# Attention scores from turned gathered rows, head products loaded over ScalarE's queue, and scatters that wait for landings

## The chip, the core and the metric

The kernel runs on one core of one Trainium2 chip. A core has TensorE (PE), VectorE (DVE), ScalarE (ACT), GpSimd (POOL) and SyncE (SP), each with its own instruction stream. They meet over semaphores; transfers go through 16 DMA engines. The metric is the device time of one execution in microseconds (us), as a median over runs.

## What is computed

Four graph layers one after the other on 3125 nodes of 64 values and 100000 edges sorted by destination: attention over four heads, two Chebyshev convolutions, messages with edge values, and a second kind of attention over 2048 nodes. The change touches the first layer, its preparation, and a re-sorting of the edge values for the third.

```python
h = jnp.maximum(_layernorm(x, axis=-1), 0.0)
# layer 0
Q = (h @ Wq).reshape(n, H, D)
K = (h @ Wk).reshape(n, H, D)
V = (h @ Wv).reshape(n, H, D)
score = jnp.einsum('ehd,ehd->eh', Q[src], K[dst]) / np.sqrt(D)
attn = jax.nn.softmax(score, axis=1)
m = V[src] * attn[:, :, None]
h_new = jax.ops.segment_sum(m, dst, num_segments=n)
...
# layer 2
message = jax.nn.relu(node_feats[edge_index[1]] + edge_feats)
message_reduce = jax.ops.segment_sum(message, edge_index[0], num_segments=num_nodes)
```

## The kernel before

The score of an edge and head is the product of the source's row h with a row that depends on the destination alone, h[dst] times a 64x64 matrix per head. `front` (the preparation) computes these head products for all nodes, 25 blocks of 128. In each block TensorE turns the rows (L661), ScalarE copies them (L584), TensorE multiplies (L667), and ScalarE and VectorE split the result into three bf16 parts (L588, L434, L590, L439). They go to the table `r3` in memory, node by node. TensorE and VectorE count edges for the later layers in the same loop.

`attend` then handles 100 items: 1000 edges each, eight tiles of 125, whose destinations lie in a window of nodes. Its loop does two items per turn, and most buffers (`spot`, `edges`, `rwin`, `hsrc`) have two slots. Per item:

- SyncE reads two numbers of the item (L760, L761) and issues four loads: `spot`, the item's numbers (L763), `edges`, its table (L766), `rwin`, the window of `r3`, 120 pieces of 512 bytes (L779), and `dstrow`, the destinations of 1000 edges on each of 120 partitions (L772).
- POOL issues eight indirect gathers, each 125 rows of h, into `hsrc` (L807). It waits first for `ao_free`, which TensorE raises when it has weighed the item that lay in the slot.
- VectorE builds `there`, a one-hot of 120x1000 that says which window row each edge wants (L850, threshold L843). TensorE multiplies it with the window (L1031), which lays the head products of 125 edges times 256 in PSUM. VectorE multiplies these with the gathered rows (L875) and adds up over 64 values (L883); ScalarE adds up four of the sixteen sums of a half item by copies with an accumulator, each followed by a read of it (L968). After the softmax (L913, L917, L982 on ScalarE, L926 to L928) L930 lays the weights into `AO`.
- TensorE weighs the gathered rows with `AO` (L1004), sixteen records of f32 products, and counts destinations by sources (L1049) from one-hots of VectorE (`hot`, L866) and ScalarE (`lo`, L958, L961). VectorE adds the counts to a large matrix (L890). Every second item TensorE projects the sums (L1018), from `U`, which ScalarE copied (L950).

After the last item an extra set of `edges` and gathers is loaded that nobody uses.

`spread` runs the rest of layer 0 and layer 1: it exchanges pairs of blocks of the count matrix (up to 1802 us in the profile), then four propagations of 25 blocks, each block ending in L1680, then the end of the layer. Beside that the edge values for layer 2 are re-sorted: 40 chunks of two halves; for each half SyncE loads the edge values, the pairs and the places (`bring_half`: L701, L704 with 1250 pieces of 8 bytes, L706), and POOL scatters them in ten indirect transfers of 125 rows (L1254) into `sorted_edges`. After every run of five POOL raises `run` and waits for `go`, which SyncE raises in `follow` (L1188) after three increments of another semaphore. SyncE loads a half anew as soon as all ten scatters of it have landed (L1194). After chunk 23 SyncE also waits for the third propagation and then reloads part of the count matrix (`again`, 1.6 MB each, twelve times, L1200) after every chunk. Layer 2 then takes 42 message items, four groups each with one activation L1572; ScalarE loads 1 MB of sorted rows per item, when the chunk is ready. Layer 3 follows from 3177 us on.

## Time and profile before

| what | us |
|---|---|
| median of 3 runs | 3109.45 |
| lowest and highest | 3109.2, 3112.74 |
| span of the profiled execution | 3529.8 |
| preparation, in the profile | 0 to about 200 |
| attention | about 200 to 1576 |
| exchange of pairs | 1576 to about 1802 |
| propagations and the layer's end | 1802 to 2415 |
| messages of layer 2 | 2415 to 3172 |
| layer 3 | 3177 to 3530 |

Times inside the program come from one execution that the hardware profiler recorded, 420 us longer than the median. A row's busy time is the sum over its instructions, and instructions of an engine overlap a little at their ends. "issue" is time in which an engine waited for nothing that the profile shows; "remote" is a wait whose end it can't name.

### The profile page before, as it was taken

The numbers are of one execution on the slowest core, as the hardware profiler recorded it, in microseconds if no ns is written. First come the engines' busy times: TensorE is split into PE (matmuls) and PEld (weight loads), VectorE is DVE, ScalarE is ACT, GpSimd is POOL, SyncE is SP. The second block draws the span as 40 slices with busy tenths as digits, with TensorE's granted clock in tenths as the row PEclk, the third lists the DMA queues.
The fourth block names the chain that finished last, engine by engine and source line by source line (L and its number), as shares of the span: only waits on it lengthen the run. The fifth ranks groups of instructions, "written<-read, shape, count | busy, mean of one in ns | idle before, by whom it ended". The sixth has DMA issues, their size and how long they took to land. (4 is left out here: it accounts for less than half of the span.)

```text
span 3529.8 us, 59565 instructions
## 1 busy us (share of the span) xinstructions
PE 1964.1 (56%) x16222; PEld 1430.6 (41%) x16222; DVE 2235.0 (63%) x4872; ACT 1128.3 (32%) x3658; POOL 1615.5 (46%) x1665
## 2 busy tenths in 40 slices
PE   6844555555555555545766556564545445564487
PEld 5723333333333333334344435453434434554222
DVE  7877777777777777754521112134547557987899
ACT  1144555444444444533210111000001001117544
POOL 1055555555555555553666666645666562000000
PEclk9955555555555555556767677675657657985699
DMA  7912121121212222236222222215544432220000
GB/s 240 364 40 45 42 45 43 43 43 44 45 40 45 42 45 41 45 88 224 65 49 50 50 50 48 60 44 154 147 132 145 127 81 84 85 82 0 0 0 9
DMA packets 399309, 267.13 MB, mean 76 GB/s; under 512 B 321456, under 2 KB 349293, under 8 KB 399073
## 3 DMA queue, kind: packets, MB, share of 16 engines
q1 hardware_dynamic: 306278, 87.81, 11.6%
q10 hardware_dynamic: 41472, 118.96, 9.3%
q0 software_dynamic: 51488, 59.40, 6.7%
q8 instruction: 47, 0.77, 0.1%
q14 instruction: 24, 0.20, 0.0%
HBM read 158.59 MB, written 107.47 MB: 75 GB/s over the span
## 5 line engine op out<-in xcount | busy, mean ns | idle before, releaser
L1254 POOL DMA_INDIRECT sorted_edges<-r_load,r_to x800 | 818.6, 1023 | 544.9 <-SPq L1188 310.2
L807 POOL DMA_INDIRECT hsrc<-h,edges x808 | 775.7, 960 | 593.8 <-PE ps L1004 362.4
L1004 PE MATMUL ps<-AO,hsrc 125*64 125x64 f32 x1616 | 195.9, 316 | 309.9 <-remote 254.3
L1049 PE MATMUL ps<-hot,lo 125*128 125x400 bf16 (+2 forms) x1000 | 272.8, 455 | 100.5 <-DVE hot L866 79.9
L1004 PEld LDWEIGHTS ps<-AO,hsrc 125*64 125x64 f32 x1616 | 180.0, 224 | 345.8 <-issue 345.8
L1031 PE MATMUL ps<-rwin,there 120*125 120x256 bf16 x800 | 183.2, 404 | 235.3 <-DVE there L850 220.0
L875 DVE TENSOR_TENSOR prod<-ps,hsrc 125x1024 f32<-125x1024 f32 x200 | 244.3, 1222 | 105.1 <-issue 101.0
L1572 ACT ACTIVATE w_work<-w_work 128x384 f32<-128x384 f32 (+1 forms) x160 | 85.8, 536 | 701.5 <-DVE w_work L1773 530.4
L866 DVE TENSOR_SCALAR hot<-ramp,small 125x400 bf16<-125x400 int16 x800 | 211.9, 322 | 148.0 <-issue 142.7
L1426 PE MATMUL ps<-R 128*128 128x64 bf16 x3000 | 156.6, 218 | 184.5 <-DVE R L1762 115.9
L1031 PEld LDWEIGHTS ps<-rwin,there 120*125 120x125 bf16 x800 | 145.1, 209 | 274.1 <-issue 274.1
L1680 DVE TENSOR_REDUCE c_red<-ps 128x64 f32<-128x192 f32 x100 | 35.7, 357 | 346.1 <-remote 220.5
L968 ACT ACTIVATE prod<-prod 125x64 f32<-125x64 f32 x800 | 194.3, 245 | 166.8 <-issue 89.4
L958 ACT ACTIVATE lo<-ramp,edges 125x128 bf16<-125x128 int16 x808 | 246.8, 388 | 0.0
L1366 PE MATMUL ps<-R,A 128*128 128x192 bf16 x1250 | 164.0, 294 | 99.3 <-issue 98.7
L1426 PEld LDWEIGHTS ps<-R 128*128 128x128 bf16 x3000 | 132.2, 114 | 206.5 <-DVE R L1762 137.5
L1049 PEld LDWEIGHTS ps<-hot,lo 125*128 125x128 bf16 x1000 | 132.4, 137 | 195.0 <-DVE hot L866 97.9
L1436 PE MATMUL ps<-w_work 128*128 128x64 bf16 x1000 | 142.3, 213 | 112.0 <-DVE R L1781 76.7
L1773 DVE TENSOR_TENSOR w_work<-ps,w_work 128x384 f32<-128x384 f32 (+1 forms) x160 | 91.4, 571 | 170.8 <-remote 160.9
L883 DVE TENSOR_REDUCE small<-prod 125x12 f32<-125x768 f32 x200 | 189.9, 949 | 3.4
L1366 PEld LDWEIGHTS ps<-R,A 128*128 128x128 bf16 x1250 | 134.4, 117 | 129.2 <-issue 124.3
L1436 PE MATMUL ps<-R,w_work 128*128 128x64 bf16 x2000 | 156.0, 215 | 42.8 <-issue 42.5
(412 smaller groups left out, 4187.1 us busy)
## 6 DMA issues: line engine op xcount, KB each, us to landing
w_work<-sorted_edges ACTq DMA_DIRECT2D x42, 1000.0 KB
r_load<-in_edge_attr_dram SPq DMA_DIRECT2D x80, 312.5 KB
dstrow<-dst_rows SPq DMA_DIRECT2D x101, 234.4 KB
sorted_edges<-A ACTq DMA_DIRECT2D x10, 2000.0 KB, 9.7
A<-counts SPq DMA_DIRECT2D x12, 1600.0 KB
counts<-A ACTq DMA_DIRECT2D x4, 4000.0 KB, 29.8
sorted_edges<-A ACTq DMA_DIRECT2D x15, 1000.0 KB, 9.5
hsrc<-h,edges POOLq DMA_INDIRECT x808
```

Source lines behind the costliest of these rows:

```text
L807: g.indirect_dma_start(out=hsrc[:, s, t, :], out_offset=None, in_=S.h0[:, :], in_offset=bass.IndirectOffsetOnAxis(ap=edges.bitcast(I32)[:, ...
L866: v.tensor_scalar(hot[0:TP, t, :], S.ramp[0:TP, OFF[t] * NB:OFF[t] * NB + SK], key[:, t:t + 1], None, ALU.is_equal).then_inc(q["hot"], 1)
L875: v.tensor_tensor(prod[0:TP, :].rearrange("p (t h f) -> p t h f", t=HT, h=H), S.ps[0:TP, hf * 1024:(hf + 1) * 1024].rearrange("p (t h f) - ...
L958: op = nc.scalar.activation(lo[0:TP, s, t, :], S.ramp[0:TP, 0:P], ACT.Square, bias=edges[0:TP, s, 3, t:t + 1])
L968: op = nc.scalar.activation(prod[0:TP, c * D:(c + 1) * D], prod[0:TP, c * D:(c + 1) * D], ACT.Copy, accum_out=score[:, hf * HT * H + c:hf ...
L1004: mm = pe.matmul(sums.rearrange("d (h w) -> d h w", h=H)[:, :, OFF[t]:OFF[t] + SUB], hsrc[0:TP, s, t, :], AO[0:TP, t, :, :], start=(t == 0 ...
L1031: mm = pe.matmul(S.ps[0:TP, t * 256:(t + 1) * 256], there[:, t * TP:(t + 1) * TP], rwin[:, s, :], start=True, stop=True, skip_group_check= ...
L1049: mm = pe.matmul(S.ps[:, at0 + c0:at0 + c1], lo[0:TP, s, t, :], hot[0:TP, t, c0 - k0:c1 - k0], start=(t == FIRST[k]), stop=False, skip_gro ...
L1254: g.indirect_dma_start(out=S.sorted, out_offset=bass.IndirectOffsetOnAxis(ap=to[:, hf, t:t + 1], axis=0), in_=load[:, hf, t, :], in_offset ...
L1366: mm = pe.matmul(S.bank[m][:, 0:SP3 * D], block_at(j, i * UN + m), part[:, j * SP3 * D:(j + 1) * SP3 * D], start=(j == 0), stop=(j == NB - 1))
L1426: mm = pe.matmul(S.bank[2 + k][:, b * D:(b + 1) * D], ohT[:, k, b * P:(b + 1) * P], hw[:, s1, d, :], start=(d == 0), stop=(d == SP3 - 1))
L1436: mm = pe.matmul(acc[:, GROUPS[n][0] + b, :], lo[:, k, b, :], mp[d][:, k, b, :], start=False, stop=False, skip_group_check=True)
```

## The change

Three parts.

In `front` the table of head products becomes `rt`, f32, turned: 128 partitions (64 values, twice), four heads, all nodes. TensorE multiplies in the other order, two products of 128 columns per block instead of one of 256; one copy by ScalarE per block replaces the split. The store is eight transfers instead of two. The list of destinations for `dstrow` isn't made any more.

In `attend` the loop does four items per turn (Q), with four slots for `spot`, `edges` and `hsrc`. Neither `there` nor `dstrow` exists. TensorE turns the gathered rows, two tiles at a time (`turn`), ScalarE copies them out of PSUM into `hT`, and TensorE multiplies each tile's rows with the part of the window in which its destinations lie, 16 nodes times four heads: eight f32 products with 64 inner values and 64 columns. VectorE multiplies these with `at`, a small one-hot of 16 that it has anyway, and adds up over 16. The window is loaded by ScalarE, 512 pieces of 160 bytes. The gathers' semaphores are one per half item. The extra gathers at the end are gone.

In `spread` POOL no longer asks SyncE. It waits by itself for the landing of the run of five before the one just issued (not after the first five of a chunk). The reloads of the count matrix come after all chunks, as does the wait for the third propagation.

```diff
-            def rem(b):
-                v.wait_ge(q["hi"], b + 1)
-                v.tensor_tensor(rest[:, b % KQ, :], S.bank[4 + b % 3][:, 0:H * D], R3[:, b, 0, :], ALU.subtract).then_inc(q["rem"], 1)
-            def low(b):
-                v.wait_ge(q["mid"], b + 1)
-                v.tensor_tensor(R3[:, b, 2, :], rest[:, b % KQ, :], R3[:, b, 1, :], ALU.subtract).then_inc(q["lo"], 1)
...
+            def kept(b0, b1):
+                act.wait_ge(q["rt"], b1)
+                for half in range(2):
+                    for k in range(2):
+                        act.dma_start(S.rt[half * D:(half + 1) * D, k:H:2, PAD + b0 * P:PAD + b1 * P],
+                                      RT[k * D:(k + 1) * D, :, b0 * P:b1 * P]).then_inc(q["stored"], 16)
...
-                    act.copy(R3[:, c, 0, :], S.bank[4 + c % 3][:, 0:H * D]).then_inc(q["hi"], 1)
-                    act.wait_ge(q["rem"], c + 1)
-                    act.copy(R3[:, c, 1, :], rest[:, c % KQ, :]).then_inc(q["mid"], 1)
+                    act.copy(RT[:, :, c * P:(c + 1) * P], S.bank[4 + c % 3][:, 0:2 * P].rearrange("p (k n) -> p k n", k=2)
+                             ).then_inc(q["rt"], 1)
...
+            with g.Fori(0, quads_of(g)) as j:
+                for s in range(Q):
+                    i = j * Q + s
+                    g.wait_ge(landed[s], j * 16 + 16)
+                    g.wait_ge(q["ao_free"], i + 1)
+                    g.sem_inc(q["carrier"], 1)
+                    for t in range(T):
+                        g.indirect_dma_start(out=hsrc[:, s, t, :], out_offset=None, in_=S.h0[:, :],
+                                             in_offset=bass.IndirectOffsetOnAxis(ap=edges.bitcast(I32)[:, s, 4, t:t + 1], axis=0)
+                                             ).then_inc(got[s][t // HT], 16)
...
-                v.tensor_scalar(there[:, :], dstrow[:, :], thr[0:KW, :], None, ALU.is_equal).then_inc(q["there"], 1)
...
-                        v.tensor_tensor(prod[0:TP, :].rearrange("p (t h f) -> p t h f", t=HT, h=H),
-                                        S.ps[0:TP, hf * 1024:(hf + 1) * 1024].rearrange("p (t h f) -> p t h f", t=HT, h=H),
-                                        hsrc[0:TP, s, HT * hf:HT * (hf + 1), :].unsqueeze(2).to_broadcast(four),
-                                        ALU.mult).then_inc(q["scores_free"], 1)
-                    def sums(hf):
-                        v.wait_ge(q["scores_free"], 2 * i + hf + 3)
-                        return own.did(v.tensor_reduce(score[:, hf * HT * H:(hf + 1) * HT * H - BYACT],
-                                                       prod[0:TP, 0:HT * H * D - BYACT * D].rearrange("p (c f) -> p c f", f=D), AX.X, ALU.add))
...
+                    v.wait_ge(q["ao"], i + 1)
+                    own.step(v.tensor_tensor(at[0:TP, :, :], S.ramp[0:TP, 0:SUB].unsqueeze(1).to_broadcast([TP, T, SUB]),
+                                             over(near[0:TP, 1, :], [TP, T, SUB]), ALU.is_equal))
+                    v.wait_ge(q["scores"], i + 2)
+                    for r in range(2):
+                        v.tensor_tensor(prod[0:TP, r:T:2, :, :], scores_at(odd, r).rearrange("p (u h w) -> p u h w", u=HT, h=H),
+                                        at[0:TP, r:T:2, :].unsqueeze(2).to_broadcast([TP, HT, H, SUB]), ALU.mult).then_inc(q["scores_free"], 1)
+                    v.wait_ge(q["scores_free"], 2 * i + 6)
+                    own.step(v.tensor_reduce(s4, prod[0:TP, :, :, :], AX.X, ALU.add))
...
+            def window(s, seen):
+                act.wait_ge(spotted[s], seen)
+                act.sem_inc(q["carrier"], 1)
+                b = act.value_load(spot[0:1, s, 1:2], min_val=0, max_val=LASTB)
+                act.dma_start(rwin[:, s % 2, :, :], S.rt[:, :, bass.ds(b, W)]).then_inc(q[f"rwin{s % 2}"], 16)
...
-                for c in range(HT * H - BYACT, HT * H):
-                    op = nc.scalar.activation(prod[0:TP, c * D:(c + 1) * D], prod[0:TP, c * D:(c + 1) * D], ACT.Copy,
-                                              accum_out=score[:, hf * HT * H + c:hf * HT * H + c + 1])
-                op.then_inc(q["summed"], 1)
...
+            with act.Fori(0, quads_of(act)) as j:
+                for s in range(Q):
+                    i, odd = j * Q + s, s % 2
+                    after, seen = (s + 1) % Q, j * 16 + 16 + 16 * ((s + 1) // Q)
+                    act.wait_ge(q["turned"], i + 1)
+                    act.wait_ge(q["scores"], i + 1)
+                    act.copy(hT[:, :, :], S.bank[2 + odd][:, 0:HT * TP].rearrange("p (u e) -> p u e", u=HT)).then_inc(q["moved"], 1)
+                    rows(i + 1, after, seen)
+                    window(after, seen)
+                    bring_sums(i, j * (Q // 2) + s // 2, odd)
                     act.wait_ge(q["soft"], i + 1)
                     nc.scalar.activation(expo, score, ACT.Exp).then_inc(q["expo"], 1)
...
+            def turn(n, s, j):
+                pe.wait_ge(q["moved"], n + 1)
+                for u in range(HT):
+                    if u % 2 == 0:
+                        pe.wait_ge(got[s][u // 2], j * (16 * HT) + 16 * HT)
+                    mm = pe.transpose(S.bank[2 + s % 2][:, u * TP:(u + 1) * TP],
+                                      hsrc[0:TP, s, 2 * u:2 * u + 2, :].rearrange("p t f -> p (t f)"), S.ident[0:TP, 0:TP])
+                mm.then_inc(q["turned"], 1)
+            n = quads_of(pe)
             with pe.Fori(0, n) as j:
-                for s in range(2):
-                    i = j * 2 + s
-                    pe.wait_ge(q["there"], i + 2)
-                    pe.wait_ge(q[f"rwin{s}"], j * 16 + 16)
+                for s in range(Q):
+                    i, odd = j * Q + s, s % 2
+                    pair = j * (Q // 2) + s // 2
+                    if s == 0:
+                        turn(i, s, j)
+                    pe.wait_ge(q[f"rwin{odd}"], pair * 16 + 16)
+                    pe.wait_ge(q["scores_free"], 2 * i + 2)
+                    pe.wait_ge(q["moved"], i + 3)
                     for t in range(T):
-                        if t % HT == 0:
-                            pe.wait_ge(q["scores_free"], 2 * i + t // HT + 1)
-                        mm = pe.matmul(S.ps[0:TP, t * 256:(t + 1) * 256], there[:, t * TP:(t + 1) * TP], rwin[:, s, :],
-                                       start=True, stop=True, skip_group_check=True)
-                        if t % HT == HT - 1:
-                            mm.then_inc(q["scores"], 1)
-                    pe.wait_ge(q["scores"], 2 * i + 2)
-                    pe.sem_inc(q["window_free"], 1)
-                    weigh(i, 1 - s)
-                    pe.wait_ge(q["lo"], i + 3)
+                        rows = slice(t % 2 * D, t % 2 * D + D)
+                        mm = pe.matmul(scores_at(odd, t % 2)[:, t // 2 * H * SUB:(t // 2 + 1) * H * SUB], hT[rows, t // 2, :],
+                                       rwin[rows, odd, :, OFF[t]:OFF[t] + SUB], start=True, stop=True, skip_group_check=True)
+                    mm.then_inc(q["scores"], 1)
+                    if s < Q - 1:
+                        turn(i + 1, s + 1, j)
+                    weigh(i, (s - 1) % Q)
...
-    STRIDE = 3
-    AFTER = 23
+    AFTER = 16
...
-            def follow(c, hf):
-                for r in range(RUNS // 2):
-                    sp.wait_ge(qr["run"], c * RUNS + hf * (RUNS // 2) + r + 1)
-                    for _ in range(STRIDE):
-                        sp.sem_inc(qr["step"], 1)
-                    sp.sem_inc(qr["go"], 1)
             def both(c):
                 for hf in range(2):
-                    follow(c, hf)
-                    sp.wait_ge(qr[f"sc{hf}"], c * (16 * HALF) + 16 * HALF)
+                    for r in range(RUNS):
+                        sp.wait_ge(qr[f"sc{hf}{r}"], c * (16 * RUN) + 16 * RUN)
                     sp.sem_inc(qr["ready"], 1)
...
+            with sp.Fori(AFTER, C2 - 1) as c:
+                both(c)
+            for hf in range(2):
+                for r in range(RUNS):
+                    sp.wait_ge(qr[f"sc{hf}{r}"], C2 * 16 * RUN)
+                sp.sem_inc(qr["ready"], 1)
             sp.wait_ge(props[3]["prod"], NB)
             with sp.Fori(0, NB // TAKE) as c:
-                both(c + AFTER)
                 again(c * TAKE)
-            with sp.Fori(AFTER + NB // TAKE, C2 - 1) as c:
-                both(c)
             sp.dma_start(counts[:, NB - 1], S.counts[NB - 1].rearrange("k p n -> p k n")).then_inc(q["again"], 16)
-            for hf in range(2):
-                follow(C2 - 1, hf)
-                sp.wait_ge(qr[f"sc{hf}"], C2 * 16 * HALF)
-                sp.sem_inc(qr["ready"], 1)
...
-                                             in_=load[:, hf, t, :], in_offset=None).then_inc(qr[f"sc{hf}"], 16)
-                        if t % RUN == RUN - 1:
-                            g.sem_inc(qr["run"], 1)
-                            g.wait_ge(qr["go"], c * RUNS + hf * (RUNS // 2) + t // RUN + 1)
+                                             in_=load[:, hf, t, :], in_offset=None).then_inc(qr[f"sc{hf}{t // RUN}"], 16)
+                        if t == HALF - 1:
+                            g.wait_ge(qr[f"sc{hf}0"], c * (16 * RUN) + 16 * RUN)
+                            g.sem_inc(qr["carrier"], 1)
+                        elif t == RUN - 1 and hf == 1:
+                            g.wait_ge(qr["sc01"], c * (16 * RUN) + 16 * RUN)
                             g.sem_inc(qr["carrier"], 1)
```

ScalarE, one item in the attention's loop, before: from the copy of U over the partial sums to the exp.

```order
L949 REGISTER_ALU [waits a_u]
L950 ACT_TABLE_LOAD
L950 COPY U<-ps 64x4x39 [waits a_proj]
L965 ISA
L966 REGISTER_ALU [waits a_scores_free]
L968 ACTIVATE prod,small<-prod 125x64 [waits a_summed]
L968 ACTIVATE prod,small<-prod 125x64 x3
L965 REGISTER_ALU
L966 REGISTER_ALU [waits a_scores_free]
L968 ACTIVATE prod,small<-prod 125x64 [waits a_summed]
L968 ACTIVATE prod,small<-prod 125x64 x3
L982 ACTIVATE small<-small 125x32 [waits a_soft]
```

After: the same engine and place; `rt` is the turned table, `hT` the turned gathered rows.

```order
L907 ACT_TABLE_LOAD [waits a_scores]
L907 COPY hT<-ps 128x500 [waits a_turned]
...
L894 ACTIVATE lo<-ramp,edges 125x128 [waits a_lo_free]
L894 ACTIVATE lo<-ramp,edges 125x128 x7
L897 ACTIVATE lo<-lo,ones 125x1024 [waits a_squares]
L886 TENSOR_LOAD spot [waits a_spot1]
...
L887 DMA rwin<-rt 128x4x40
L875 ISA [waits a_u]
L876 COPY U<-ps 64x4x39 [waits a_proj]
L912 ACTIVATE small<-small 125x32 [waits a_soft]
```

The eight L968 are gone; a copy of turned rows stands first, and the load of the next item's window stands ahead of the copy of U and the exp.

TensorE, second item of the turn, before: the score products from window and one-hot, then the weighing.

```order
L1030 ISA [waits a_hot_free,a_rwin1,a_there]
L1031 MATMUL ps<-rwin,there 125x256 [waits a_scores_free]
L1031 MATMUL ps<-rwin,there 125x256 x3
L1030 REGISTER_ALU
L1031 MATMUL ps<-rwin,there 125x256 [waits a_scores_free]
L1031 MATMUL ps<-rwin,there 125x256 x3
L1004 MATMUL ps<-AO,hsrc 64x4x16 [waits a_scores,a_ao,a_u_free]
L1004 MATMUL ps<-AO,hsrc 64x4x16 x7
```

After: the same place; `ident` is the identity matrix for the transposes.

```order
L970 ISA [waits a_hot_free,a_rwin1]
L974 MATMUL ps<-rwin,hT 125x64 [waits a_moved,a_scores_free]
L974 MATMUL ps<-rwin,hT 125x64 x7
L958 MATMUL ps<-ident,hsrc 128x125 [waits a_got20,a_moved]
L958 MATMUL ps<-ident,hsrc 128x125
L958 MATMUL ps<-ident,hsrc 128x125 [waits a_got21]
L958 MATMUL ps<-ident,hsrc 128x125
L934 MATMUL ps<-AO,hsrc 64x4x16 [waits a_ao,a_u_free]
```

The products wait for ScalarE's copy (`a_moved`) and the window instead of the one-hot, and the next item's transposes stand between them and the weighing.

POOL, the scatter loop, first half and the start of the second, before.

```order
L1254 DMA sorted_edges<-r_load,r_to 230528x80 [waits landed0]
L1254 DMA sorted_edges<-r_load,r_to 230528x80 x4
L1258 ISA
L1254 DMA sorted_edges<-r_load,r_to 230528x80 [waits r_go]
L1254 DMA sorted_edges<-r_load,r_to 230528x80 x4
L1258 REGISTER_ALU
L1254 DMA sorted_edges<-r_load,r_to 230528x80 [waits r_go,landed1]
```

After: the whole loop.

```order
L1184 DMA sorted_edges<-r_load,r_to 230528x80 [waits landed0]
L1184 DMA sorted_edges<-r_load,r_to 230528x80 x9
L1187 ISA
L1184 DMA sorted_edges<-r_load,r_to 230528x80 [waits r_sc00,landed1]
L1184 DMA sorted_edges<-r_load,r_to 230528x80 x4
L1184 DMA sorted_edges<-r_load,r_to 230528x80 [waits r_sc01]
L1184 DMA sorted_edges<-r_load,r_to 230528x80 x4
L1179 REGISTER_ALU [waits r_sc10]
```

The waits for SyncE's `r_go` after every five are replaced by waits for `r_sc..`, the landing of a run of five.

## Rows read from the trace of the kernel before

**Rows 1.** The page: busy time by engine; GB/s moved in 40 slices of 88 us.

```profile
PE 1964.1 (56%) x16222; PEld 1430.6 (41%) x16222; DVE 2235.0 (63%) x4872; ACT 1128.3 (32%) x3658; POOL 1615.5 (46%) x1665
...
GB/s 240 364 40 45 42 45 43 43 43 44 45 40 45 42 45 41 45 88 224 65 49 50 50 50 48 60 44 154 147 132 145 127 81 84 85 82 0 0 0 9
```

**Rows 2.** All instances of line L1004's weight load, 400 to 1300 us: ns min/median/max, first, last.

```profile
L1004 PEld LDWEIGHTS ps<-AO,hsrc x1072: 178/227/232, 403.2 to 1296.8; 125*64 125x64 f32 x179
```

**Rows 3.** Us, busy us of PE, PEld, DVE, ACT, POOL, then granted clock, DMA share, GB/s.

```profile
400.00:1300.00 900.00, 472.11 (x2535) 336.34 (x2534) 668.02 (x1763) 448.68 (x1832) 511.66 (x535) 0.56 0.20 43
```

**Rows 4.** Groups of instructions by line, attention, 400 to 1300 us: busy us, mean ns.

```profile
L875 DVE TENSOR_TENSOR prod<-ps,hsrc 125x1024 f32<-125x1024 f32 x133 | 162.5, 1222 | 68.2 <-issue 64.6 <-DMA hsrc<-h,edges 1.5 <-remote 1.4
...
L968 ACT ACTIVATE prod<-prod 125x64 f32<-125x64 f32 x532 | 129.2, 245 | 109.8 <-issue 59.2 <-DVE prod L875 50.5
L883 DVE TENSOR_REDUCE small<-prod 125x12 f32<-125x768 f32 x133 | 126.3, 949 | 2.3
...
L890 DVE TENSOR_TENSOR A<-A,ps 128x500 f32 (+1 forms) x132 | 86.6, 656 | 0.0
...
L850 DVE TENSOR_SCALAR there<-dstrow,thr 120x1000 bf16<-120x1000 int16 x66 | 32.9, 499 | 2.3
```

**Rows 5.** Waits, 400 to 1300 us: engine and line, released by; us, times, longest.

```profile
POOL hsrc L807 <- PE ps L1004: 242.7, 66, 5.0
```

**Rows 6.** Timeline, attention: start us, us, engine, line; in brackets the wait before.

```profile
703.91 0.94 POOL L807 DMA_INDIRECT hsrc<-h,edges  x1 [4.88 <-PE ps L1004]
705.15 0.94 POOL L807 DMA_INDIRECT hsrc<-h,edges  x1 [0.30 <-issue]
...
700.73 1.03 DVE L866 TENSOR_SCALAR hot<-ramp,small 125x400 bf16<-125x400 int16 x4 [2.87 <-issue]
...
711.66 0.71 SPq L779 DMA_DIRECT2D rwin<-r  x1
...
712.59 1.94 PE L1004 MATMUL ps<-AO,hsrc 125*64 125x64 f32 x16 [0.87 <-issue]
...
721.00 1.96 PE L1031 MATMUL ps<-rwin,there 120*125 120x256 bf16 x8 [0.30 <-DVE there L850]
```

**Rows 7.** Timeline of scatters and of SyncE's issues, beside the propagations.

```profile
2041.84 0.97 POOL L1254 DMA_INDIRECT sorted_edges<-r_load,r_to  x1 [2.52 <-SPq L1188]
2043.11 0.97 POOL L1254 DMA_INDIRECT sorted_edges<-r_load,r_to  x1 [0.30 <-issue]
...
2051.79 0.00 SPq L701 DMA_DIRECT2D r_load<-in_edge_attr_dram  x1
...
2055.16 2.49 SPq L706 DMA_DIRECT2D r_to<-places  x1
```

**Rows 8.** Waits of POOL from 1802 to 2940 us, after the exchange of the pairs.

```profile
POOL sorted_edges L1254 <- SPq L1188: 243.3, 66, 30.5
```

**Rows 9.** Line L1572, four instances per message item, beside scatters and after them.

```profile
L1572 ACT ACTIVATE w_work<-w_work x87: 522/523/578, 2416.8 to 2894.7; 128x384 f32<-128x384 f32 x65, 128x448 f32<-128x448 f32 x22
...
L1572 ACT ACTIVATE w_work<-w_work x61: 522/523/578, 2961.6 to 3158.6; 128x384 f32<-128x384 f32 x46, 128x448 f32<-128x448 f32 x15
```

**Rows 10.** Line L561, copies out of PSUM, in the preparation.

```profile
L561 ACT COPY f_edges<-ps x6: 404/496/586, 22.6 to 26.0; 125x512 f32<-125x512 f32 x3, 125x288 f32<-125x288 f32 x3
```

**Rows 11.** All issues of line L704 by SyncE, ns min/median/max.

```profile
L704 SPq DMA_DIRECT2D r_load<-edge_pairs x80: 459/2556/26997, 1539.0 to 2913.2; - x80
```

**Rows 12.** Timeline of POOL at the attention's end.

```profile
1560.98 0.95 POOL L807 DMA_INDIRECT hsrc<-h,edges  x1 [10.75 <-DMA edges<-edge_table]
```

**Rows 13.** Groups by line, preparation, 0 to 200 us: busy, mean ns, wait before.

```profile
L590 ACT CAST A<-A 128x256 bf16<-128x256 f32 x25 | 10.2, 406 | 22.5 <-DVE A L434 22.5
```

**Rows 14.** All scatters, line L1254: ns min/median/max, first and last start.

```profile
L1254 POOL DMA_INDIRECT sorted_edges<-r_load,r_to x800: 965/971/2474, 1576.7 to 2938.6; - x160
```

**Rows 15.** Line L1680, one instance per block of a propagation, in two stretches.

```profile
L1680 DVE TENSOR_REDUCE c_red<-ps x67: 345/358/359, 1859.5 to 2287.7; 128x64 f32<-128x192 f32 x67
...
L1680 DVE TENSOR_REDUCE c_red<-ps x6: 357/357/358, 2349.5 to 2359.8; 128x64 f32<-128x192 f32 x6
```

287 lines of the change are left out of this document (105 added, 182 removed).

## The prediction

> **What bounds the kernel now.** I read the engine totals first [rows 1]. VectorE (DVE) is the busiest engine, at 63% of the span, and GpSimd (POOL), which does little but issue indirect transfers, works through two long stages: the gathers of the attention and the scatters after it. The last 350 us are layer 3, which no edit touches. So three stretches are to be priced: the attention, the scatters with the propagations beside them, and the messages that follow.
>
> The attention does 100 items. Product L1004 has 16 records per item, so its 1072 records from 403.2 to 1296.8 are 67 items, about 13.5 us each [rows 2]. Nobody is full in that time: the window of 900 us, 66.7 items, has VectorE busy 668 us, 10.0 per item, ScalarE 449, 6.7, and TensorE 472, 7.1 [rows 3]. Half of VectorE's time is in lines that the change removes: two products L875 (2.44), two reductions L883 (1.90) and the one-hot L850 (0.50), 4.8 us [rows 4]. The rest of the item is a ring of waits. POOL is held 242.7 us by L1004 [rows 5], since it has two gather buffers and must see one weighed before it fills it again. At each loop turn, every second item, VectorE stands some 3 us before L866 by "issue", which is no wait on anybody [rows 6]. The same group shows POOL's own rate: gathers start 1.25 us apart, so eight take 10.0 us. That is the floor under everything below.
>
> In the scatter stage the starts are 1.27 us apart, ten to a half chunk, 12.75 us, but a half begins with a wait for SyncE, 2.52 us in the example [rows 7] and 243.3 us from the exchange of the pairs on [rows 8], since SyncE's answers (L1188) stand behind its own loading of the next half, 5.9 us from the issue of L701 to the end of L706's [rows 7].
>
> The messages come in four activations L1572 per item. While scatters run, 87 of them take 2416.8 to 2894.7, 22 us an item; after the last scatter 61 take 2961.6 to 3158.6, 13.1 us [rows 9].
>
> **The attention after the change.** VectorE loses the 4.8 us and gets two products of 125x256 from PSUM and one reduction of 512 to 32. The nearest rows are in [rows 4]: L890, 500 columns with one operand in PSUM in 0.656 us, gives 0.36 each; L883, 768 columns in 0.949, gives 0.65. That makes 10.0 - 4.8 + 0.7 + 0.65 = 6.6 us. ScalarE loses eight L968 of 0.245, 2.0 us, with their reads of the sum, and gets the copy of the turned rows, 0.59 by L561 [rows 10], a register load and the issue of the window: 6.7 - 2.0 + 0.6 = 5.3 plus the issue. TensorE swaps L1031's 1.96 us for eight f32 score products and four f32 transposes. L1004, eight f32 products too, does its sixteen records in 1.94 us [rows 6]; I take 1.9 and, for half as many, 1.0. TensorE has 7.1 - 2.0 + 2.9 = 8.0 us. SyncE loses the window and the line of destinations and keeps two issues per item. All are under 10.0, and four gather buffers let POOL run up to three items ahead of L1004, so its waits of [rows 5] go and it sets the item: 10.0 us. **100 x (13.5 - 10.0) = 350 us.**
>
> The window's issue, moved to ScalarE, is the one unknown price: 512 pieces of 160 bytes. SyncE's issues bound it from both sides: the window of before, 120 pieces, 0.71 us [rows 6]; pair loads of 1250 pieces of 8 bytes, median 2.6, worst 27.0 [rows 11]. I take 1.5, nearer the first by pieces. ScalarE then has 6.8 of 10 us, and POOL's 10.0 hides it. On its queue the copy of U, the exp and the next copy of turned rows stand behind that issue; VectorE waits for the exp, TensorE for the copies.
>
> At the end, before, an extra set of eight gathers starts at 1560.98 behind the last item, and the stage stays open for it [rows 12]. It is gone: **10 us**. In the preparation the three-way split goes (L434, L439, L588, L590 for 25 blocks; ScalarE waited 22.5 us for L434 before L590 [rows 13]). TensorE counts edges in the same stretch and is next, with two products per block instead of one. I book **5 us**, between 0 and 20. The stores are more and smaller in sum, off the path.
>
> **The scatters.** POOL no longer asks SyncE. After a run of five it waits for the landing of the run before, whose last transfer was issued five starts, 6.4 us, earlier. The wait at a half's start now ends with the loading of that half, which begins when its last scatter has landed and needs 5.9 us, while the other half scatters for 12.75: 6.8 us are left for the two landings. So the 243 us go, and the scatters need 1362 - 243 = 1119 us from the end of the attention instead of 1362 (1576.7 to 2938.6 [rows 14]). They are not alone on the path. The propagations and the layer's end take 840 us from the attention's end (1576) to the first message (2416.8), beside the scatters, and I leave that as it is. Then messages: 279 us at 22 us are 12.7 items, the other 27.3 take 13.1 each, 358 us. From the attention's end to the last message 840 + 279 + 358 = 1477, against 1596 (1576 to 3158.6, and 13 for that item's end). **119 us.** The reloading of the counts, 12.5 transfers of 1.6 MB, lay between chunks and now comes behind the last scatter: at the 364 GB/s of the busiest slice [rows 1] 55 us of transfers, beside 358 us of messages. It hides, or costs up to 25 us by late loads; I book nothing.
>
> **The sum.** 350 + 10 + 5 + 119 = 484 us off a profiled span of 3529.8. That execution is 420 us longer than the median of 3109.45, so not all of it is there to be saved. If all parts shrink alike (3109.45/3529.8 = 0.881), 426 remain: 2683. The 3 us per loop turn before L866, 1.5 per item, may be the recording's doing, since no semaphore ends them; if they are, 150 of the 350 were never in the median, and (484 - 150) x 0.881 = 294 remain: 2815. Nothing in the profile decides between the two. I take the middle, **2745 us**.
>
> The Trainium skill, "TensorE: Matmul & The Clock Gate" (Part 3: Packing small matmuls), says that a weight load overlaps running products only when their row groups differ. L1004 uses the same rows every time; its sixteen loads of 0.227 us [rows 2] would then need 3.6 us, and the timeline has 1.94 for all sixteen records [rows 6]: the trace disagrees, and the measurement decides. By the rule the transposes would cost 1.8 instead of 1.0, and TensorE's sum would be 8.8 instead of 8.0.
>
> **Rivals.** *A, TensorE's chain becomes the bound.* The scores hang on a chain that L1004 doesn't have: gathers, transposes, copy, products, reduction, exp, AO, on engines that each work in order. If the score products show their weight loads, 16 x 0.22 = 3.5 us instead of 1.9, TensorE has 9.6 of 10 us, and with 1.5 us of such waits an item takes 11.1: 110 x 0.881 = 97 of the gain are lost, about 2845. For it: the granted clock is 0.56 on the average here [rows 3], mostly the lower level of 1.2 GHz. Against it: [rows 6]. Chance 0.15.
>
> *B, the scatter stage gives nothing.* POOL's wait for a landing is as long as the one it replaces, or the denser scatters slow the propagations and the messages' loads by what they gain: 119 x 0.881 = 105 less, about 2850. For it: the last reductions L1680 of a propagation, six blocks, come 2.1 us apart with the scatters held up (2349.5 to 2359.8), and 67 before them 6.5 apart [rows 15]; and messages beside scatters take 22 us. Chance 0.13.
>
> *C, slower: the window's issue holds ScalarE.* In rows: ScalarE has 5.3 us of other work, so the item grows past 10.0 from an issue of 4.7 us, past 13.5 from 8.2, and the kernel is slower than before from about 9.5, where also the 134 us of the other stages are used up. Issues of 27 us exist, where the queue is full [rows 11]; at 12 us an item takes 17.3 and the kernel 0.881 x (380 - 134) = 217 us more than before, 3326. Against it: 512 pieces in 10 us are fewer than the 1250 of L704 in 15, which cost 2.6. Chance 0.04. The Trainium skill, "DMA: Bandwidth & Descriptors" (Specifications), puts the size for full rate at 512 bytes and has smaller pieces read, changed and written; the window goes from 512-byte pieces to 160-byte ones. No run here shows a window of such pieces.
>
> *D, more than forecast.* The 3 us per turn are real and go, and gathers, timed here with recording, are quicker without: 2600 to 2660. Chance 0.13.
>
> **How the numbers follow.** Forecast (2660 to 2820) 0.52, A 0.15, B 0.13, D 0.13, C 0.04, and 0.03 for within 0.2% of before, where some order of waits keeps the item at 13 us. About 0.2%, 6 us, is what a measurement of this kernel can tell from no change. Faster 0.93, same 0.03, slower 0.04. The range takes in A, B and most of D: 2620 to 2880.
>
> **What the profile after would show.** Right: eight gathers 10.0 us apart per item without a wait for a weighed buffer; scatters in an unbroken 1.27 us step over the borders of halves; some 12 message items before the last scatter. Wrong: POOL idle before gathers, with ScalarE's issue of the window over 5 us (C) or score products over 3 us (A); waits at each run of five, or the reductions of the propagations further apart than before (B).

## The result, and the profile after

| kernel | median us | range | runs |
|---|---|---|---|
| before | 3109.56 | 3109.2 to 3112.74 | 4 |
| changed | 2803.0 | 2798.81 to 2806.05 | 4 |

The ratio is 0.9004, with a 95% interval of 0.899 to 0.9018: 307 us faster. The time lies within the range of the prediction (2620 to 2880), 58 us above the predicted 2745. Two terms behind that number were far off, in opposite directions.

One thing has to be said before any rows are compared. The rows read ahead of the prediction come from an execution with a span of 3529.8 us, 420 above the median. The changed kernel's traced execution has a span of 2801.8, as long as its median. So the kernel before was traced once more (first experiment below), and that span is 3122.3. The two traces of the same code differ in idle time that no semaphore ends, for example before VectorE's L866, here in the page of the first and of the second:

```profile
L866 DVE TENSOR_SCALAR hot<-ramp,small 125x400 bf16<-125x400 int16 x800 | 211.9, 322 | 148.0 <-issue 142.7
```

```profile
L866 DVE TENSOR_SCALAR hot<-ramp,small 125x400 bf16<-125x400 int16 x800 | 214.7, 328 | 0.7 <-DVE small L851 0.7
```

From here on "before" means the second trace; the first is cited by its groups of rows. The second is still 13 us longer than the median, so the differences by stage add up to some 320 us (3122.3 - 2801.8) and not to 307.

Busy time by engine, the page of the changed kernel, against [rows 1]:

```profile
PE 1767.1 (63%) x17472; PEld 1308.5 (47%) x17472; DVE 1921.8 (69%) x4516; ACT 925.8 (33%) x2108; POOL 1637.8 (58%) x1656
```

The attention, 300 to 1200 us. The columns are the stretch, its length, busy us of PE, PEld, DVE, ACT and POOL, then the granted clock, the DMA share and GB/s. First the changed kernel, then the second trace of before; this answers [rows 3]:

```profile
300.00:1200.00 900.00, 600.70 (x4445) 423.35 (x4446) 632.51 (x2089) 427.64 (x1088) 683.51 (x711) 0.68 0.21 36
```

```profile
300.00:1200.00 900.00, 549.97 (x3105) 392.62 (x3105) 810.47 (x2166) 547.95 (x2241) 622.91 (x654) 0.62 0.25 53
```

All gathers, with what their engine waited for before them (us, times), changed and before:

```profile
L775 POOL DMA_INDIRECT hsrc<-h,edges x800: 940/944/1428, 203.9 to 1215.9; - x160
...
  issue: 236.7, 777
  PE ps L934: 6.1, 20
```

```profile
L807 POOL DMA_INDIRECT hsrc<-h,edges x808: 938/944/1375, 202.0 to 1328.4; - x162
...
  issue: 208.8, 675
  PE ps L1004: 128.1, 98
```

From the first to the last gather it is 1012 us for 100 items, 10.1 each, and 1126.4 us for 101 sets, 11.15 each. In the changed kernel 237 us of POOL's idle time are the 0.30 us between two issues, and only 6.1 a wait for a weighed buffer (128.1 before; [rows 5] has 242.7 for the first trace). VectorE was busy 810 of 900 us before and is busy 633 now.

All scatters, changed and before, the same view; [rows 14] and [rows 8] are their counterparts:

```profile
L1184 POOL DMA_INDIRECT sorted_edges<-r_load,r_to x800: 963/967/2460, 1238.8 to 2369.0; - x160
...
  issue: 225.7, 739
  DMA r_to<-places: 47.8, 25
  DMA sorted_edges<-r_load,r_to: 11.0, 36
```

```profile
L1254 POOL DMA_INDIRECT sorted_edges<-r_load,r_to x800: 962/967/2470, 1335.0 to 2725.5; - x160
...
  SPq L1188: 341.8, 78
```

2369.0 - 1238.8 = 1130 us against 2725.5 - 1335.0 = 1391. The 342 us of waits for SyncE are gone, and 48 us now end with the loading of a half. Most of these 48 are one old wait under a new name: during the exchange of the pairs POOL stands 37.3 us, where it stood 41.6 before, because SyncE is held there by two issues of the loading, 27.25 and 14.43 us long (changed kernel):

```profile
1257.49 27.25 SPq L681 DMA_DIRECT2D r_load<-edge_pairs  x1
1284.79 14.43 SPq L683 DMA_DIRECT2D r_to<-places  x1
...
1301.33 0.97 POOL L1184 DMA_INDIRECT sorted_edges<-r_load,r_to  x1 [37.31 <-DMA r_to<-places]
```

The step of the scatters is not an unbroken 1.27 us, as the prediction said it would be. The median scatter takes 0.967 us, the mean 1.059, and from 1800 to 2000 us the mean is 1.127, with single ones of 1.7. 800 steps of 1.27 would be 1016 us; the rest of the 1130 is some 74 us of longer scatters and the waits. What makes those scatters longer is open. Before, the same stretch has a mean of 1.150.

The reductions of the propagations, one per block, changed and before; see [rows 15]:

```profile
L1612 DVE TENSOR_REDUCE c_red<-ps x100: 345/357/359, 1420.1 to 1710.7; 128x64 f32<-128x192 f32 x100
```

```profile
L1680 DVE TENSOR_REDUCE c_red<-ps x100: 343/357/359, 1528.0 to 1817.3; 128x64 f32<-128x192 f32 x100
```

100 blocks take 291 and 289 us, 2.9 each: denser scatters don't slow them. The 67 blocks of [rows 15] had 6.5 us each.

The activations of the messages, changed and before; see [rows 9]:

```profile
L1504 ACT ACTIVATE w_work<-w_work x160: 522/523/577, 1755.6 to 2404.0; 128x384 f32<-128x384 f32 x120, 128x448 f32<-128x448 f32 x40
...
  SPq L1126: 87.6, 6
```

```profile
L1572 ACT ACTIVATE w_work<-w_work x160: 522/523/578, 1862.7 to 2751.9; 128x384 f32<-128x384 f32 x120, 128x448 f32<-128x448 f32 x40
...
  SPq L1195: 377.2, 17
```

The last one starts 35 us after the last scatter, and 26 us before the change. In the kernel before, 377 us of ScalarE's idle time end with SyncE's word (L1195) that a chunk is ready: the messages followed the scatters. In the changed kernel it is 87.6 us in six waits (L1126), none of them before 2200 us. Until then the messages run at their own pace, though scatters run beside them: 88 activations, 22 items, in 304 us, 14.0 each. So the end of the scatters sets the end of the messages in both kernels, but now only some 104 us of such waits are left (87.6, and 16.5 for the last chunk). By an estimate from these rows, still faster scatters could give about that much and no more.

What stands on the path after them, changed kernel: SyncE's issues (L1131, L1166 the reloads of the counts, L1169 the last rows to be added) and VectorE at L1729:

```profile
2371.61 43.69 SPq L1131 DMA_DIRECT2D A<-counts  x12
...
2420.77 0.53 SPq L1169 DMA_DIRECT2D w_work<-sorted_edges  x1
...
2433.30 0.24 DVE L1729 TENSOR_SCALAR w_work<-w_work 128x25 bf16<-128x25 f32 x1 [26.15 <-DMA w_work<-sorted_edges]
```

Twelve issues of reloads take 43.7 us, a thirteenth (L1166) 3.7; the last rows are asked for only at 2420.8 and VectorE waits 26.15 us for them.

### The profile page after: what moved, and what is told of

It is laid out like the page before. It is cut to its first block and busy times, and to the rows that moved or that the text cites. A ratio compares the mean times of both kernels' runs of the same rounds, so it can differ in the third digit from the quotient of the medians.

```text
span 2801.8 us, 56861 instructions
## 1 busy us (share of the span) xinstructions
PE 1767.1 (63%) x17472; PEld 1308.5 (47%) x17472; DVE 1921.8 (69%) x4516; ACT 925.8 (33%) x2108; POOL 1637.8 (58%) x1656
## 5 line engine op out<-in xcount | busy, mean ns | idle before, releaser
L1184 POOL DMA_INDIRECT sorted_edges<-r_load,r_to x800 | 847.3, 1059 | 284.5 <-issue 225.7
L958 PE MATMUL ps<-ident,hsrc 125*128 125x125 f32 x400 | 102.8, 361 | 228.1 <-DMA hsrc<-h,edges 228.1
L1368 PEld LDWEIGHTS ps<-w_work 128*128 128x128 bf16 x1000 | 105.1, 109 | 261.7 <-DVE w_work L1710 252.5
L815 DVE TENSOR_TENSOR A<-A,ps 128x500 f32 x200 | 123.5, 660 | 95.0 <-PEq L994 95.0
L934 PE MATMUL ps<-AO,hsrc 125*64 125x64 f32 x1616 | 181.0, 298 | 2.6 <-DVE AO L847 2.6
L1709 DVE TENSOR_TENSOR R<-w_work 128x384 f32<-128x384 f32 (+1 forms) x160 | 92.4, 577 | 124.2 <-ACT w_work L1504 115.2
L934 PEld LDWEIGHTS ps<-AO,hsrc 125*64 125x64 f32 x1616 | 163.0, 205 | 27.7 <-issue 25.7
L2057 PE MATMUL ps<-R,Z 128*65 128x512 f32 (+1 forms) x350 | 151.8, 564 | 35.8 <-DVE R L2097 35.8
L958 PEld LDWEIGHTS ps<-ident,hsrc 125*128 125x128 f32 x400 | 49.4, 171 | 256.6 <-DMA hsrc<-h,edges 238.7
L974 PE MATMUL ps<-rwin,hT 64*125 64x64 f32 x1600 | 125.3, 301 | 58.7 <-ACT hT L907 31.4
L1710 DVE TENSOR_TENSOR w_work<-w_work 128x768 bf16<-128x768 bf16 (+1 forms) x160 | 157.4, 984 | 0.0
L974 PEld LDWEIGHTS ps<-rwin,hT 64*125 64x125 f32 x1600 | 111.8, 211 | 97.2 <-issue 58.0
```

What stands on the lines that cost most here:

```text
L934: mm = pe.matmul(sums.rearrange("d (h w) -> d h w", h=H)[:, :, OFF[t]:OFF[t] + SUB], hsrc[0:TP, s, t, :], AO[0:TP, t, :, :], start=(t == 0 ...
L958: mm = pe.transpose(S.bank[2 + s % 2][:, u * TP:(u + 1) * TP], hsrc[0:TP, s, 2 * u:2 * u + 2, :].rearrange("p t f -> p (t f)"), S.ident[0: ...
L974: mm = pe.matmul(scores_at(odd, t % 2)[:, t // 2 * H * SUB:(t // 2 + 1) * H * SUB], hT[rows, t // 2, :], rwin[rows, odd, :, OFF[t]:OFF[t] ...
L1184: g.indirect_dma_start(out=S.sorted, out_offset=bass.IndirectOffsetOnAxis(ap=to[:, hf, t:t + 1], axis=0), in_=load[:, hf, t, :], in_offset ...
L1368: mm = pe.matmul(acc[:, GROUPS[n][0] + b, :], lo[:, k, b, :], mp[d][:, k, b, :], start=False, stop=False, skip_group_check=True)
L1710: v.tensor_tensor(lo[:, k, 0:m, :], ramp1b.unsqueeze(1).to_broadcast([P, m, P]), over(slo[:, s, cols], [P, m, P]), ALU.is_equal).then_inc( ...
```

## The experiments

**A second trace of the kernel before**, unchanged.

> The kernel before, unchanged, for a second trace of it. Its page in hand has a span 420 us above the median, the changed kernel's page has none of that. If the recording itself holds the engines (theory), the trace again lies some 400 us above 3110, with propagation reductions 5 to 6 us apart; if that page was an odd execution (rival), the span is now about 3108, an attention item takes about 12 us (100 items in 1200), a block of a propagation 2.7 us as in the changed kernel, and the stages can be compared one by one.

Measured: 3124.03 us (3107.92 to 3133.47) against 3111.18 beside it, ratio 1.0025 (0.9998 to 1.0051), so the same kernel to within its noise. Of its page:

```profile
span 3122.3 us, 59565 instructions
...
L1254 POOL DMA_INDIRECT sorted_edges<-r_load,r_to x800 | 829.8, 1037 | 562.3 <-SPq L1188 341.8
```

The rival holds: 59565 instructions recorded, as in the first page, and no general slowness. Recording alone doesn't hold the engines; what did in the first traced execution stays open. One trail: there the engines' own small instructions are irregular too. A register move of SyncE at L779 takes up to 1.4 us, against 0.03 in the second trace, and the issue of the window 0.70 us as a median, against 0.33. The expected 12 us per item was itself too high: it is 11.15.

**Each half alone.** The first takes the second function (`spread`) of the changed kernel and leaves preparation and attention as before, the second is the other way round; no line was edited.

> The scatter stage alone: preparation and attention as before, the second function as after. My sum gave this part 119 us on the profile's scale, 105 on the median's: 3005. Rival: in the median the scatters never waited that long for SyncE, or the late reload of the counts gives it back: 3060 to 3110. Other rival: the parts help each other and this alone gives more than 150.

> Preparation and attention alone as after, the scatter stage as before. If the item goes from about 12.0 to 10.1 us, this is 190 + 10 + 5 = 205 us: 2905. If the item took 13.5 before also without the recording: 350, 2760. Together with the run of the scatter stage alone the parts should add up to the 306 measured, if each acts in its own stretch.

Measured: the scatter stage alone 2899.59 us, ratio 0.9308 (0.9288 to 0.9328), **212 us**. Preparation and attention alone 3022.24, ratio 0.9698 (0.9676 to 0.972), **89 us**. Together 301 of the 307: the halves act each in its own stretch. Both theories missed, with the sizes the wrong way round: 105 and 205 us were expected. Scatters of the first, gathers and scatters of the second kernel:

```profile
L1244 POOL DMA_INDIRECT sorted_edges<-r_load,r_to x800: 962/968/2476, 1335.8 to 2466.2; - x160
```

```profile
L775 POOL DMA_INDIRECT hsrc<-h,edges x800: 940/945/1409, 212.7 to 1223.6; - x160
```

```profile
L1194 POOL DMA_INDIRECT sorted_edges<-r_load,r_to x800: 962/968/2459, 1245.6 to 2627.4; - x160
...
  SPq L1128: 332.3, 79
```

Scatters take 1130 to 1141 us wherever the new waits are, and 1379 to 1391 with the old ones. The preparation is not shorter: over all the traces the first gather starts between 201.1 and 212.7 us where it is the new one (without the run with six gathers, which clears more first), and between 201.8 and 205.7 where it is the old one. No run separates the parts of the attention's change, the new products and the four slots.

**The place of the reloads.**

```diff
-            with sp.Fori(AFTER, C2 - 1) as c:
-                both(c)
+            with sp.Fori(AFTER, LATER) as c:
+                both(c)
+            sp.wait_ge(props[3]["prod"], NB)
+            with sp.Fori(0, NB // TAKE) as c:
+                both(c + LATER)
+                again(c * TAKE)
+            with sp.Fori(LATER + NB // TAKE, C2 - 1) as c:
+                both(c)
...
-            sp.wait_ge(props[3]["prod"], NB)
-            with sp.Fori(0, NB // TAKE) as c:
-                again(c * TAKE)
```

`LATER` is 23.

> The changed kernel with the reload of the counts back between chunks 23 to 34, and the wait for the third propagation ahead of it. In the changed kernel VectorE waits 26.2 us for the last rows (L1729), whose load is issued behind the reload, and 2.7 for the gather after it. Theory: the reload there costs 26 to 29 us, and this kernel takes 2803 - 27 = 2776. Rival: 20.8 MB between the chunks delay the scatters and the messages' loads by as much: 2795 to 2810.

Measured: 2778.67 us (2774.55 to 2782.4), ratio to before 0.8925 (0.8905 to 0.8945), 24 us less than the changed kernel. As expected, and the scatters aren't slower by more than 11 us (2374.4 - 1233.7 = 1141):

```profile
L1188 POOL DMA_INDIRECT sorted_edges<-r_load,r_to x800: 962/968/2482, 1233.7 to 2374.4; - x160
```

This is the fastest of all kernels here.

**The old answers with late reloads**, to see whether the answers or the reloads were the cause.

```diff
+            def follow(c, hf):
+
+                for r in range(RUNS):
+                    sp.wait_ge(qr["run"], (c * 2 + hf) * RUNS + r + 1)
+                    for _ in range(3):
+                        sp.sem_inc(qr["step"], 1)
+                    sp.sem_inc(qr["go"], 1)
...
                 for hf in range(2):
+                    follow(c, hf)
...
-                        if t == HALF - 1:
-                            g.wait_ge(qr[f"sc{hf}0"], c * (16 * RUN) + 16 * RUN)
+                        if t % RUN == RUN - 1:
+                            g.sem_inc(qr["run"], 1)
+                            g.wait_ge(qr["go"], (c * 2 + hf) * RUNS + t // RUN + 1)
                             g.sem_inc(qr["carrier"], 1)
```

> The changed kernel with the old answers of SyncE in the scatter loop, but the reload of the counts still behind the last scatter. With the runs at hand it fills the square: new waits and late reload 2803, new waits and early reload 2779, old answers and early reload 3022. If the answers alone carry the gain and the reload's place costs 24 us in both, this is 3046. Rival: the old kernel's reloads between chunks were what delayed SyncE's answers, and the gain is partly theirs: 2950 to 3020.

Measured: 3051.32 us (3039.13 to 3055.15), ratio to before 0.9798 (0.9754 to 0.9842). The theory had 3046. The square is 3022 / 3051 with the old answers and 2779 / 2803 with the new waits: the answers cost 243 to 248 us, the late reloads 24 to 29, and the two add. POOL waited 322.7 us for SyncE:

```profile
L1194 POOL DMA_INDIRECT sorted_edges<-r_load,r_to x800: 962/967/2460, 1233.9 to 2612.6; - x160
...
  SPq L1127: 322.7, 79
```

**The answer ahead of the loads.** From the last kernel: it keeps the whole exchange of `run`, `step` and `go`, and only moves the answer to the first run of the next half ahead of the reloading.

```diff
                 for hf in range(2):
-                    follow(c, hf)
+                    answer(c, hf, 1)
                     for r in range(RUNS):
                         sp.wait_ge(qr[f"sc{hf}{r}"], c * (16 * RUN) + 16 * RUN)
                     sp.sem_inc(qr["ready"], 1)
+                    answer(c + hf, 1 - hf, 0)
                     bring_half(nc, I, S, sp, c + 1, hf)
```

> As the run with old answers and late reload (3051), but SyncE answers the first run of the next half before it issues that half's reloading (5.9 us), not after. Theory: GpSimd's 4 us waits per half are for SyncE, which stands in its own issues. With the answer ahead, the loads end some 13.3 us after a half's end and the half is ready at about 15, against 12.75 of scatters, so 1 to 2.5 us per half remain as a wait for the loads: 80 x (4.1 - 1.8) = 180 less, 2870 (2820 to 2930). Rival: the waits belong to the handshake as such, or to the landings of the scatters: no change, 3030 to 3060.

Measured: 2809.4 us (2803.1 to 2814.29), ratio 0.9032 (0.9004 to 0.906). The whole gain is back, more than the theory allowed (2870, 2820 to 2930), and the kernel is level with the changed one (0.9004, 0.899 to 0.9018). Its waits (engine and line, released by, us, times, longest):

```profile
POOL sorted_edges L1198 <- DMA r_to<-places: 48.6, 17, 37.2
...
POOL sorted_edges L1198 <- SPq L1127: 9.2, 27, 1.2
```

The timeline of before shows the place. POOL's waits end about 1 us after SyncE's last issue of a half (L706) is through:

```profile
1605.83 0.97 POOL L1254 DMA_INDIRECT sorted_edges<-r_load,r_to  x1 [3.68 <-SPq L1188]
...
1617.26 0.96 POOL L1254 DMA_INDIRECT sorted_edges<-r_load,r_to  x1 [0.30 <-issue]
1620.66 0.96 POOL L1254 DMA_INDIRECT sorted_edges<-r_load,r_to  x1 [2.44 <-SPq L1188]
...
1613.34 0.27 SPq L701 DMA_DIRECT2D r_load<-in_edge_attr_dram  x1
1613.79 2.96 SPq L704 DMA_DIRECT2D r_load<-edge_pairs  x1
1616.93 2.57 SPq L706 DMA_DIRECT2D r_to<-places  x1
```

At 1617.26 + 0.96 POOL asks; SyncE issues until 1616.93 + 2.57 = 1619.50 and then answers; POOL goes on at 1620.66. So the wait stands in the middle of a half, after its first five. The prediction had it at the half's start, from the same kind of rows: ten starts lie between two waits either way. What I had left as a remaining wait of 1 to 2.5 us for the loads isn't there: 9.2 us for SyncE in all.

**One more VectorE instruction per item**, before and after: a reduction over 1000 constants whose result nobody uses.

```diff
                     products(0)
+                    own.did(v.tensor_reduce(junk[0:TP, 0:1], S.ramp[0:TP, 0:1000], AX.X, ALU.max))
                     keys(4, 8)
```

```diff
+                    v.wait_ge(q["junk"], i)
+                    v.tensor_reduce(junk[0:TP, 0:1], S.ramp[0:TP, 0:1000], AX.X, ALU.max).then_inc(q["junk"], 1)
                     v.wait_ge(q["ao"], i + 1)
```

> The kernel before with one more VectorE reduction per item, over 1000 constants, about 1.2 us, whose result nobody uses. Theory: VectorE sets the item before the change (busy 810 of 900 us in the new trace of it), so 100 items cost 100 to 120 us more: 3210 to 3235. Rival: GpSimd's ring with two gather buffers sets it, and 0.5 us per item of room is there: 3130 to 3170.

> The changed kernel with the same extra VectorE reduction per item. Theory: GpSimd sets the item at 10.0 us and VectorE has 3 us of room: 2803 to 2815. Rival: the ring through VectorE is as long as GpSimd's ten us, and the 1.2 us show at once: 2880 to 2925.

Measured: before with it 3207.93 us (3195.6 to 3212.16), ratio 1.0294 (1.025 to 1.0338), 98 us more, just under what was expected; changed with it 2822.17 us (2816.99 to 2831.45), 19 more than 2803.0 and 7 above the upper end. As ratios to before they are 0.9068 (0.9028 to 0.9107) with it and 0.9004 (0.899 to 0.9018) without. The instruction takes 1.18 us in both. The gathers of the two:

```profile
L808 POOL DMA_INDIRECT hsrc<-h,edges x808: 938/944/1380, 205.7 to 1425.2; - x162
```

```profile
L776 POOL DMA_INDIRECT hsrc<-h,edges x800: 940/944/1460, 206.5 to 1228.2; - x160
```

Items of 12.07 instead of 11.15 us, and 10.22 instead of 10.12. Before, 0.92 of 1.18 us go through, so VectorE's order of work sets the item; after, 0.10 go through. In the spans, 22 us apart, that is 9.7 us. The first gather starts 2.6 later, the way from the last gather to the first scatter is 4.4 longer, and the scatters take 4.9 more (1135.1 us); the first of these three lies within what the other traces differ by, the other two are not explained. The window of the second kernel shows VectorE at 719 of 900 us and POOL as before:

```profile
300.00:1200.00 900.00, 583.91 (x4395) 410.27 (x4396) 719.44 (x2156) 424.18 (x1077) 685.71 (x704) 0.71 0.20 36
```

**Six gathers per item instead of eight**, in the changed kernel. The rows of the last two tiles of each item are zero, so its sums are not those of the layer; GpSimd clears all four slots first, and the gathers start some 11 us later (214.8 against 203.9).

```diff
-                    for t in range(T):
+                    for t in range(T - 2):
                         g.indirect_dma_start(out=hsrc[:, s, t, :], out_offset=None, in_=S.h0[:, :],
```

> The changed kernel with six gathers per item instead of eight; the rows of the last two tiles stay zero, so 250 of 1000 edges of an item are weighed with zeros (its time alone is of use). Theory: GpSimd's issue sets the item in the changed kernel, 8 x 1.25 = 10.0 of 10.1 us. Six need 7.5; VectorE's lines take 7.0 of 10.1 us and TensorE's 6.7, so the item falls to 7.8 to 8.8 us and the kernel to 2570 to 2680. Rival: the ring of TensorE, ScalarE and VectorE (transposes, copy, products, exp, weighing) sets the item by itself: 9.8 to 10.1 us, 2770 to 2803.

Measured: 2659.51 us (2655.99 to 2670.9), ratio to before 0.8541 (0.851 to 0.8573), 143 us less than the changed kernel and within what was expected. Gathers and window:

```profile
L776 POOL DMA_INDIRECT hsrc<-h,edges x600: 938/944/1462, 214.8 to 1073.1; - x150
...
  issue: 165.3, 534
  PE ps L935: 110.9, 62
```

```profile
300.00:1000.00 700.00, 520.16 (x4024) 382.79 (x4023) 562.12 (x1892) 388.19 (x984) 468.00 (x483) 0.74 0.20 35
```

1073.1 - 214.8 over 100 items is 8.6 us. So the issue of the gathers does set 10.1, and the next limit is 8.6, not the 7.5 of six gathers: POOL waits 110.9 us for a weighed buffer again. There VectorE is busy 0.80 of the time and TensorE 0.74, and neither is full. Which chain of waits makes the 8.6 us is not shown.

No run has fewer slots than four. With two, the kernel would stand still: each item's transposes are queued on TensorE ahead of the weighing of the item before, which would have to free their slot. Whether three would do as well as four is open.

## Why the prediction was right, and where it wasn't

**The number** was within its range by luck, because two errors cancelled. On the median's scale the sum had some 190 to 320 us for preparation, attention and its end, and about 105 for the scatter stage. The runs gave 89 and 212. (The middle of 2683 and 2815 is 2749; the prediction has 2745.)

**The item after the change** was predicted at 10.0 us, set by POOL; it is 10.1, and the runs with six gathers and with the extra reduction show that POOL sets it. This step held, with the floor read from eight gathers 1.25 us apart.

**The item before** is the step that failed: "about 13.5 us each" and "nobody is full in that time". It is 11.15 us, and VectorE is nearly full: 810 of 900 us busy, 10.0 us per item. That figure was the same in the trace in hand, 668 of 900 over 66.7 items ([rows 3]). So 3.5 of the 13.5 us were no work of the fullest engine, and I booked all of them as gain: 350 us, where 100 items gave 105. Even the lower estimate, which took out only the 3 us per turn of VectorE's "issue" gaps ([rows 6]), kept 12.0. The other waits of that trace were longer as well: POOL's for L1004 are 242.7 us there and 98.7 in 300 to 1200 us of the second.

**The terms of the engines.** VectorE was to have 6.6 us per item after the change; 633 of 900 us are 7.1. The two products of 256 columns out of PSUM take 0.42 us each, not 0.36, which is 0.12 of the missing 0.5; the rest is in small lines. ScalarE was to have 5.3 us and has 4.8. TensorE's terms, with the timeline of the changed kernel (start, us, engine, line, op):

```profile
850.67 1.09 PE L974 MATMUL ps<-rwin,hT 64*125 64x64 f32 x16
851.69 0.43 PE L958 MATMUL ps<-ident,hsrc 125*128 125x125 f32 x2
853.61 0.68 PE L958 MATMUL ps<-ident,hsrc 125*128 125x125 f32 x2 [1.49 <-DMA hsrc<-h,edges]
854.22 1.97 PE L934 MATMUL ps<-AO,hsrc 125*64 125x64 f32 x16
...
861.05 1.15 PE L934 MATMUL ps<-AO,hsrc 125*64 125x64 f32 x16
...
1135.96 0.56 ACTq L887 DMA_DIRECT2D rwin<-rt  x1
```

Sixteen score records (L974) take 1.09 us, against 1.9 booked, the transposes (L958) 0.43 and 0.68 for two each, against 1.0 for four. The granted clock is 0.68 in this stretch instead of 0.62, a mean between the levels of 1.2 and 2.4 GHz. The sixteen records of L934 take 1.97 us at 854.22 and 1.15 at 861.05, where [rows 6] has 1.94 for its counterpart; over all items they average 1.8. TensorE has 6.8 us per item (600.7 of 900) where 8.0 were predicted, so rival A did not come. Its score products average 1.25 us per item, not 3.5.

The prediction weighed the rule of the Trainium skill, "TensorE: Matmul & The Clock Gate" (Part 3: Packing small matmuls), that a weight load overlaps running products only when their row groups differ, and found that the trace disagrees. The rows don't show that. It multiplied one load's 0.227 us by sixteen, but the loads' records overlap one another: the sixteen of L934 at 854.22 lie within 1.78 us, those at 861.05 within 1.01. Such durations can't be added up, and whether a load overlaps running products on the same rows stays open here. Only the price per sixteen records is shown.

The window's issue by ScalarE (L887) is 0.56 us, with 0.67 the longest of 101; I had booked 1.5 between 0.71 and 2.6. No wait of TensorE ends with the window's landing, and rival C fell with it. C named a full queue as the cause of the 27 us issue; the traces show only where it stands, in the exchange of the pairs.

**The end and the preparation.** 10 and 5 us were booked. From the first gather to the first scatter it is 1035 us against 1133, 98 less, where 100 items at 1.05 make 105: nothing of the 10 is left, since the changed kernel still has its last item to score and weigh after the last gather, 23 us, while before the extra gathers ran beside that and 7 us were left. The preparation, booked at 5, gave nothing that the traces can tell.

**The scatters** were predicted at 1119 us instead of 1362, and are 1130 instead of 1391: 260 gained for 243. Right in size. The reason was right too (SyncE's answers behind its own loading), and the run with the answer ahead shows it; the place of the wait was wrong, it stands after the first five of a half.

**What follows them** is the second failing step: "they are not alone on the path", 840 us of propagations and then 22 us per message item. Both came from the disturbed trace. Without it the first message starts 528 us after the attention's end, not 840, and the messages then wait for chunks. Some 12 message items were to come before the last scatter, and 38 of 40 do (152 of the 160 activations). Of the 260 us, 252 arrive at the last message (2751.9 - 1335.0 = 1417 against 2404.0 - 1238.8 = 1165). **Rival B** argued from the same rows and falls with them: propagation blocks are 2.9 us apart in both kernels, and messages beside scatters take 14.0 us, not 22.

**The reloads** were booked at nothing, "or up to 25 us by late loads". They cost 24 to 29. I had thought of the messages' loads; the one that suffers stands behind the reloads in SyncE's own queue, the last rows, asked for only after 49 us of issues (2371.6 to 2420.8). The change gathers the reloads directly ahead of L1169, and the prediction never asked what stood behind them.

**Rival D** was to come from quicker gathers and a real stall per turn. Gathers take 0.944 to 0.947 us as a median in all traces; the stall wasn't there. The chances given to A, B and D (0.41 together) leaned on rows of one disturbed execution: its granted clock, its slow propagations and messages, its stall.

## What to carry to other kernels

When a trace's span is far above the median, look for one quantity that doesn't depend on idle time, the busy time per item of the fullest engine, and bound the period with it before booking any waits as gain; better, get a second trace. An engine that both answers another engine and issues loads should answer first: here a handshake that looked like 250 us of cost cost nothing once its answer stood ahead of some 6 us of issues. And a load moved "behind everything" still has something behind it on its own queue.

## What the runs showed that was not expected

- Two traced executions of the same program can differ by 13%: 3529.8 and 3122.3 us, with 100 propagation blocks in 561 and 289 us. The cause is open. The spans of all ten other traced executions lie within 0.5% of their kernels' medians.
- GpSimd's issue of a gather of 125 rows takes 0.944 us as a median, with 0.30 to the next, in every trace of before and after (0.947 in the disturbed one). A scatter takes 0.967 and 0.30, but stretches with a mean of up to 1.15 exist. The two stages that are made of these issues take 1012 and 1130 of the changed kernel's 2803 us. That the issue sets the first was tested by taking gathers away; for the second it is read from POOL's waits.
- SyncE is held for 43.7 us by the issue of twelve transfers of 1.6 MB, 3.6 each on average, where a load of a half chunk holds it 6.2 (1613.34 to 1619.50), and 42 us during the exchange of the pairs.
